# Edge sums of a segment moved behind its first fill of counts, and their placing behind the third

## The reference

```python
h = node_features @ W_node.T + b_node
e = edge_features @ W_edge.T + b_edge
msg = h[src] + e
msg = msg @ W_msg.T + b_msg
s = jax.ops.segment_sum(msg, dst, num_segments=n)
deg = jax.ops.segment_sum(jnp.ones(dst.shape, msg.dtype), dst, num_segments=n)
...
x = _layernorm(x + s / jnp.maximum(deg, 1.0)[:, None], axis=-1)
```

## Time and profile before

| | |
|---|---|
| median of 3 runs | 785.0 us (783.43 to 785.41) |
| profiled execution, its own time | 783.87 us |
| its span | 782.0 us |
| mean granted clock of TensorE over the span | 0.977 |
| PE matmuls busy | 688.6 us (88%) |
| DVE busy | 630.1 us (81%) |
| ACT busy | 438.3 us (56%) |
| GpSimd (POOL) busy | 270.0 us (35%) |
| PE on the chain of work that ended last | 52% of the span |

### The profile page before, as it was taken

One profiled execution on the slowest core, in us unless ns is written; L12 is line 12 of the kernel. 1 busy time (PEld: TensorE's weight loads), 2 busy tenths in 40 slices (PEclk: granted clock), 3 DMA queues, 4 the chain that ended last, 5 costly groups with the idle time before them and its releaser, 6 DMA issues.

```text
span 782.0 us, 24842 instructions
## 1 busy us (share of the span) xinstructions
PE 688.6 (88%) x10360; PEld 620.7 (79%) x10360; DVE 630.1 (81%) x1155; ACT 438.3 (56%) x897; POOL 270.0 (35%) x210
## 2 busy tenths in 40 slices
PE   3265577899999989999999998999999999999995
PEld 3244466778888979989988987988998998989994
DVE  7989896868998878878878877789798788779822
ACT  3322496656565556556556555656665665656641
POOL 2737300301443836426426455532543542000000
PEclk9998698999999999999999999999999999999998
DMA  6953543434556574474472575464574574454000
GB/s 174 321 182 79 138 135 111 167 111 146 183 190 194 187 260 156 160 258 158 159 262 55 184 253 195 152 229 156 194 238 146 192 236 153 173 182 169 17 14 16
DMA packets 81518, 130.71 MB, mean 167 GB/s; under 512 B 12100, under 2 KB 25126, under 8 KB 81303
## 3 DMA queue, kind: packets, MB, share of 16 engines
q1 hardware_dynamic: 73230, 115.79, 44.3%
q0 software_dynamic: 7200, 12.39, 5.7%
q10 hardware_dynamic: 974, 0.90, 0.5%
HBM read 125.80 MB, written 3.23 MB: 165 GB/s over the span
## 4 chain that ended last, share of the span: by engine, by line
PE 52%; DVE 11%; issue 4%; POOL 2%; DMA 1%; DVEq 1%; ACT 0%; POOLq 0%
PE x_ps L745 29%; PE count_ps L730 10%; PE win_ps L666 8%; DVE key_hot L886 3%; DVE row_hot L886 2%; PE win_ps L673 2%; POOL x_gathered L607 2%; DMA x_gathered<-in_x_dram,x_index 1%; PE misc_ps L761 1%; PE misc_ps L762 1%; DVE y L932 1%; DVEq L863 1%; DVE y L925 1%; DVE onehot L852 1%; DVE sums_e L876 1%
## 5 line engine op out<-in xcount | busy, mean ns | idle before, releaser
L1416 ACT CAST region<-count_ps 128x490 bf16<-128x490 f32 x575 | 324.3, 573 | 192.8 <-PE count_ps L730 188.5
L745 PE MATMUL x_ps<-region,x_rest 128*128 128x250 bf16 x2254 | 413.6, 270 | 0.0
L745 PE MATMUL x_ps<-region,x_hi 128*128 128x250 bf16 x1127 | 306.2, 272 | 0.5 <-ACT region L1416 0.5
L607 POOL DMA_INDIRECT x_gathered<-in_x_dram,x_index x144 | 195.1, 1355 | 278.5 <-PE count_ps L730 258.9
L886 DVE TENSOR_TENSOR row_hot<-iota_bf,row 125x3200 bf16<-125x3200 bf16 x115 | 209.4, 1821 | 42.1 <-PE count_ps L730 29.1
L730 PE MATMUL count_ps<-key_hot,row_hot 125*128 125x98 bf16 x2875 | 224.4, 209 | 15.2 <-ACT region L1416 8.6
L745 PEld LDWEIGHTS x_ps<-region,x_rest 128*128 128x128 bf16 x2254 | 211.4, 98 | 16.2
L730 PEld LDWEIGHTS count_ps<-key_hot,row_hot 125*128 125x128 bf16 x2875 | 185.6, 99 | 37.9 <-issue 10.4
L886 DVE TENSOR_TENSOR key_hot<-iota_bf,key 125x2500 bf16<-125x2500 bf16 x115 | 167.2, 1454 | 0.0
L666 PE MATMUL win_ps<-edges,onehot 128*32 128x128 f32 x3232 | 107.2, 286 | 13.7 <-DVE onehot L852 12.1
L745 PEld LDWEIGHTS x_ps<-region,x_hi 128*128 128x128 bf16 x1127 | 109.5, 97 | 8.0 <-ACT region L1416 0.6
(11 more groups left out here) (194 smaller groups left out, 415.7 us busy)
## 6 DMA issues: line engine op xcount, KB each, us to landing
edges<-in_edge_attr_dram SPq DMA_DIRECT2D x101, 1024.0 KB, 5.8
resid<-in_x_dram SPq DMA_DIRECT2D x25, 125.0 KB
out_dram<-y SPq DMA_DIRECT2D x25, 125.0 KB
x_gathered<-in_x_dram,x_index POOLq DMA_INDIRECT x144
region<-in_dst_dram ACTq DMA_DIRECT2D x1, 768.0 KB
win_src<-in_src_dram,clipped_int POOLq DMA_INDIRECT x23, 4.4
x_index<-in_src_dram SPq DMA_DIRECT2D x9, 8.0 KB, 5.7
region<-in_L_gnn_W_node_dram SPq DMA_DIRECT2D x1, 64.0 KB
```

The lines of the kernel that those rows point to most:

```text
L607: pool.indirect_dma_start(out=x_gathered[:, i, :], out_offset=None, in_=x[:, :], in_offset=bass.IndirectOffsetOnAxis(ap=x_index[:, k, i:i ...
L745: mm = pe.matmul(x_ps[m % 2][:, 0:NB], rows, counts[m % 2][:, b, :], start=(n == 0), stop=(n == PARTS - 1))
L1416: act.copy(counts[m % 2][:, :, f * FILL * 2:(f + 1) * FILL * 2], count_ps[fill % COUNT_BANKS][:, 0:FILL * KEYS].rearrange("p (n b) -> p b ...
```

## The change

On PE a segment that has items now does the first fill (counts and their application), then the two `sum_windows`, then the second and the third fill, and behind the third `place_windows`. Before, the sums came ahead of the first fill and the placing behind the second. On ACT `copy_windows` moves in the same way, behind the move of the first bank. The five lead slots are as before, and so are DVE, GpSimd and the DMA queue.

```diff
--- before.py
+++ after.py
@@ -766,9 +766,8 @@
             pe.wait_ge(rel_copied, 2)
             for u in range(SLOTS):
                 g = u - LEAD
-                for v in items_at[u]:
-                    sum_windows(v)
                 if u < LEAD:
+                    sum_windows(u)
                     t = blocks_at[u][0]
                     place_windows(u)
                     if t == 0:
@@ -782,7 +781,9 @@
                     count_fill(g, f)
                     if m > 0:
                         apply_counts(m - 1, s * FILLS + f, ROUND_FILLS)
-                    for v in items_at[u] if f == 1 else []:
+                    for v in items_at[u] if f == 0 else []:
+                        sum_windows(v)
+                    for v in items_at[u] if f == 2 else []:
                         place_windows(v)
                     if f == 2 and s == 3 and m + 1 < ROUNDS:
                         turn_keys(m + 1)
@@ -1443,7 +1444,7 @@
                 g = u - LEAD
                 if g >= 0 and g % SEGS == 0 and g // SEGS >= 2:
                     take_x(g // SEGS - 2)
-                for v in items_at[u]:
+                for v in items_at[u] if u < LEAD else []:
                     copy_windows(v)
                 if u == ZERO_X:
                     act.wait_ge(fin_mm, ZERO_FIN)
@@ -1459,6 +1460,8 @@
                 m, s = divmod(g, SEGS)
                 for f in range(FILLS):
                     move_bank(g * FILLS + f)
+                    for v in items_at[u] if f == 0 else []:
+                        copy_windows(v)
                     if f == 4 and u - 1 in finish_at:
                         take_root(roots)
                         roots += 1
```

## The result

The changed kernel takes 796.69 us in the median (four executions, 793.23 to 798.33), the kernel before 784.25 us (783.43 to 785.41). The ratio is 1.0149, with a 95% interval from 1.0116 to 1.0183. The forecast of 785.3 us, and its range to 788.5 us, were wrong. The profiled execution has a span of 791.4 us and a time of 793.23 us; its span is 9.4 us above that of before.

The account below looks back on a forecast made before the run. The prediction took PE as the bound from 225 us, with PE and DVE taking turns from 100 to 225. Start 5.8 - gather segments 7.0 + clock 1.5 = +0.3 us on 785.0 gave 785.3 us, range 781.5 to 788.5.

Parts of the forecast that it names:

- Gather segments: Nine gather segments: the first fill shortens PE's wait for the one-hot by 0.88 us each, 7.9 us gained, 7.0 net.
- 0.9 taken back for segment 74: Segment 74: the later placing passes through DVE into the chain of gather segment 78 and cancels its 0.88 us gain.
- The argument that the one-hot comes no later: Gather rounds: DVE reaches `add_sums` in s=2 with 0.58 us to spare after the later placing, so nothing is added.
- Ordinary segments: nothing: Even stretch, s=4 and s=2: placing 0.88 us later is hidden by DVE's spare time of 1.37 and 0.58 us; cost nothing.
- the same argument was made for segments 19 and 24: Segments 19 and 24: sums no longer cover PE's wait for hots, leaving PE 4.5, then 5.8 us late.
- The lateness does fall by 0.9 us from gather segment to gather segment: Sign in the changed kernel's profile: PE's lateness falls in steps of 0.9 us from gather segment to gather segment.
- The sums of segment 63: Sign in the changed kernel's profile: these gather sums start 2 to 5 us later than at 451.38, first fill done.
- Start: Up to segment 24: later placings in 9, 12 and 14 (2.6 us) and lost cover in 19 and 24; 5.8 us lost.
- Clock: Behind PE's new waits in segments 19 and 24: one fall to half clock in two waits, 1.5 us, bounds 0 and 3.0.
- the two waits that I had priced: PE's new waits for hots at the first fills of segments 19 and 24, forecast as 2.9 and 3.2 us.
- the 3.54 us at 61.79: Wait in the kernel before, read as leaving the clock at 1.00, against a fall behind 3.24 us at 157.68.
- clock falls behind both: Rival: the clock falls behind the waits of segments 19 and 24 both; +1.8 to +3.3 us, 786.8 to 788.3; chance 0.2.

Follow-up runs that it names:

- the two experiments alone: Against the kernel before: only the placing behind the third fill everywhere, 802.77 us, ratio 1.0113; only the sums behind the first fill everywhere, 798.49 us, ratio 1.0035.
- the long one on the third chip: Longest of six executions (809.21 us) of the unaltered changed kernel, timed again beside the kernel before; median 805.80 us, ratio 1.0103.
- the kernel with the links alone: Kernel before with placings behind the third fill up to segment 24 and sums behind the first in segments 19 and 24 alone: 805.07 us, ratio 1.0112.
- the kernel before again: The kernel before, nothing changed, run once more for a trace on the chip of the experiments: 794.84 us.

## Why the prediction was wrong, step by step

The profiled spans differ by 9.4 us; the forecast had 0.3.

*Gather segments.* The wait fell by 12.1 - 4.3 = 7.8 us; forecast 7.9 (and 0.9 taken back for segment 74). The argument that the one-hot comes no later held: in the round of segment 63 the hots of s=2 start at 446.11, and `add_sums` follows at 456.59, 10.48 us behind, where it was 10.5 before. DVE's spare time shrank as foreseen (1.37 us before):

```profile
446.11 1.83 DVE L887 TENSOR_TENSOR row_hot<-iota_bf,row 125x3200 bf16<-125x3200 bf16 x1 [0.44 <-PE count_ps L730]
...
456.59 0.29 DVE L877 TENSOR_TENSOR sums_e<-sums_e,win_ps 128x128 f32 x1 [0.65 <-PE win_ps L673]
...
458.01 1.29 DVE L853 TENSOR_TENSOR onehot<-iota_bf,rel_col 128x512 f32<-128x512 bf16 x2
```

*Ordinary segments: nothing.* This is the step that failed. I looked at what a later placing does there, not at what the sums had covered, though the same argument was made for segments 19 and 24. In s=4 of rounds without a gather segment the trace after shows waits for `key_hot` of 0.72, 0.72, 1.18, 0.71 and 0.39 us, 3.7 us in all. From the round ahead to the round behind these places PE falls back by 0.9, 0.9, 1.35, 0.9 and 0.55 us, 4.6 in all, somewhat more than the idle that the list has. The later placing is not free either: twice, for 0.71 and 0.56 us, the fills wait for ACT to move a bank, and PE falls back by 0.9 and 0.7 us, 1.6 in all. Both waits are also in the kernel with only the placing later, and not in the one with only the sums later. The first, in segment 75, is the 0.9 us that I had given to gather segment 78: the late placing of segment 74 costs what was forecast, but it reaches PE through ACT, and segment 78 keeps its gain. Last, PE now reaches gathered rows earlier than they are there:

```profile
491.69 1.59 PE L666 MATMUL win_ps<-x_gathered,onehot 128*32 128x128 f32 x32 [1.96 <-DMA x_gathered<-in_x_dram,x_index]
```

There and in segment 33 these waits grow by 0.4 us each, 0.8 us in all. So 4.6 + 1.6 + 0.8 = 7.0 us of the 7.8 are given back. The lateness does fall by 0.9 us from gather segment to gather segment, as forecast, but rises in between. The sums of segment 63 show it: they start 458.76 - 451.38 = 7.4 us late, not 2 to 5.

*Start.* Without the clock, forecast 5.8 us. At the first fill of segment 25 PE is 8.6 us late. The row of before stands first, that of after second:

```profile
227.99 0.39 PE L730 MATMUL count_ps<-key_hot,row_hot 125*128 125x98 bf16 x5
```
```profile
236.59 0.39 PE L730 MATMUL count_ps<-key_hot,row_hot 125*128 125x98 bf16 x5
```

Of these, 2.0 us are clock, read by holding the same matmuls against each other (1.6 us behind the wait of segment 24, where the windows gave 1.7, and 0.4 in segment 13), which leaves 6.6. The mechanism of this term was right and its size 0.8 us too small. That the two experiments alone give 2.5 + 3.3 = 5.8 is partly luck: there PE makes up 1.1 us that it does not make up when both moves are made.

*Clock.* Forecast 1.5 us, bounds 0 and 3.0. Measured 3.6 us: 1.6 behind segment 24, 1.6 behind the wait for a DMA at 491.69, and 0.4 in segment 13, where the low clock lasted longer. For the two waits that I had priced the forecast came true, one fall in two. The term was mis-sized because it had no price for any other place. That the fall behind 491.69 comes from the change is not shown: its wait grew from 1.6 to 1.96 us, but the kernel with the sums later in segments 19 and 24 alone has a fall in segment 67, where nothing was changed and no such wait is.

That one fall in two came true was luck, since half of the argument for it was misread. I took the clock behind the 3.54 us at 61.79 for full, because the windows say 1.00. But the ten matmuls there take 1.00 us, as they do at the low clock at 90.30, and not 0.62 as at the full clock at 94.12 (both rows of the kernel before):

```profile
90.30 1.02 PE L730 MATMUL count_ps<-key_hot,row_hot 125*128 125x98 bf16 x10
...
94.12 0.62 PE L730 MATMUL count_ps<-key_hot,row_hot 125*128 125x98 bf16 x10
```

So PE was at the low clock at 61.79. The windows of this trace say 1.00 everywhere up to 72 us; in the trace of the kernel with the new order in the gather segments alone, the same instructions stand at the same place, take the same time, and the window says 0.50. So close to the start the windows cannot be relied on, and the time of the same matmuls has to be read instead.

The rival "clock falls behind both" did not come true in this execution, but it did in the long one on the third chip, behind 1.96 and 2.43 us.

By this account -7.8 + 7.0 + 6.6 + 3.6 = 9.4 us, which is all of the difference. The forecast of 0.3 us had 0.9 (segment 74) where 7.0 us are given back; these 6.1 us are the main error. The clock adds 2.1 and the start 0.8. The median was 3.5 us above the profiled execution, while it was 0.4 us above for the kernel before: other executions of the changed kernel lose more. On the first chip none of the longer ones was traced; on the third one was, and most of its excess lies in the start, with the falls of the clock named above.

The Trainium skill, "TensorE: Matmul & The Clock Gate", section "HAM oscillation — how this bites in real kernels", has the array fall back to its low clock in waits between bursts. The section speaks of long waits, and the forecast applied it to both of its waits without asking whether they were long enough. This case's traces agree behind 3.20 us; behind 4.11 us the clock was low as well. They also show that the wait behind which it falls need not be the longest: 1.96 us were enough at 491.69, and 3.05 us were not in segment 24 of the kernel with the links alone:

```profile
230.19 0.40 PE L736 MATMUL count_ps<-key_hot,row_hot 125*128 125x98 bf16 x5 [3.05 <-DVE key_hot L894]
```
```profile
230.00:236.00 6.00, 5.81 (x111) 5.20 (x112) 4.54 (x8) 2.59 (x6) 0.95 (x1) 1.00 0.38 111
```

## What to carry to other kernels

Before work is moved away from the front of a wait, hold the end of the producer against the *start* of that work in every kind of segment, not only where a wait is listed: a covered wait has no row. A reordering that pays in one kind of segment is best made there alone; here the gather segments gave 0.4%, and all segments from 25 on but the covering ones 0.7 to 0.9% (on chips where the idle inside the sums helped), while the change everywhere lost 1.0 to 1.5%. Two moves that cost 2.5 and 3.3 us alone can cost 8.6 us together: here 1.7 us of that is a fall of the clock, and 1.1 us is time that PE can make up behind one move and not behind both. And a low clock is priced by the work done in it, not by its length.

## What I had not expected of the hardware

The length of a wait did not decide whether the clock fell. Behind 1.96 us in segment 19 it fell in one kernel (0.79 over 8 us) and stayed at 1.00 in another. Nor was a fall's length fixed: behind the same wait of 3.24 us, with all the same instructions until then, the clock was 0.83 over 156 to 166 us in one execution (the kernel before again) and 0.50 in another:

```profile
156.00:166.00 10.00, 8.76 (x66) 6.94 (x70) 3.65 (x10) 2.67 (x5) 0.00 (x0) 0.50 0.03 6
```

(the kernel with the sums later in s=4 alone). From the first fill of segment 13 to that of segment 15 PE takes 20.41 us there, against 18.22: 2.2 us more by the clock. It can explain part of the spread between executions of one kernel, 8.3 us for this one (794.14 to 802.46); that it does was not tested.

The same program was 10 us longer on the chips of the experiments than on the first, with a clock that was no lower (0.982 against 0.977), for the most part because of idle stretches inside the sums that nothing releases (8.3 us of idle in 24 places). They are rarer where the sums stand behind a fill (5.0 us in the changed kernel, 2.1 us in the one with only the sums later). This can be why the same change measured 1.0149 on one chip and 1.0103 on another, but the intervals of the two ratios overlap, so even the difference is not shown.
